# First layer of a four-layer graph network: the attention product and the probability transposes change places in TensorE's order

## The reference

```python
q = split_heads(x @ Wq.T + bq)          # H = 8 heads of 32
k = split_heads(x @ Wk.T + bk)
v = split_heads(x @ Wv.T + bv)
scores = jnp.einsum('bhsd,bhtd->bhst', q, k) * SCALE
scores = jnp.where(mask, scores, jnp.float32(-1000000000.0))   # 6 static masks, 2 of adj
attn = jax.nn.softmax(scores, axis=-1)
out = jnp.einsum('bhst,bhtd->bhsd', attn, v)
out = out.transpose(0, 2, 1, 3).reshape(Bn, S, D)
return out @ Wo.T + bo
```

## Time and profile before

| | us |
|---|---|
| median of 3 runs (lowest, highest) | 2136.47 (2135.16, 2137.15) |
| the profiled execution | 2136.92 |
| its span, first to last instruction | 2135.0 |
| TensorE busy in the span | 2034.9 (95%) |
| VectorE busy | 1514.9 (71%) |
| ScalarE busy | 1001.2 (47%) |
| GpSimd busy | 566.6 (27%) |

### The profile page before, as it was taken

How to read it: one execution, slowest core, us unless ns; L and a number is a source line. 1 busy time by engine, 2 the same in 40 slices (tenths; PEclk the granted TensorE clock), 3 DMA queues, 4 the chain that set the end, 5 groups by cost and what they waited for, 6 DMA issues and landing times. The chain is left out here.

```text
span 2135.0 us, 52810 instructions
## 1 busy us (share of the span) xinstructions
PE 2034.9 (95%) x18428; PEld 1882.9 (88%) x18428; DVE 1514.9 (71%) x3344; ACT 1001.2 (47%) x2057; POOL 566.6 (27%) x624
## 2 busy tenths in 40 slices
PE   7999999899999799999999999999998899999997
PEld 6888888899998699999999999999998778887886
DVE  7899999677777455555555555555554799999997
ACT  6667666455555322232222232233222567666765
POOL 4344444222222011101111111111111444444442
PEclk9999999999999899999999999999999999999999
DMA  3222222432323200011111111001110122112211
GB/s 104 69 75 70 66 75 75 148 90 82 89 77 90 73 16 26 22 30 30 30 30 30 30 30 30 21 24 30 30 30 21 42 61 60 51 55 60 60 45 45
DMA packets 149370, 113.31 MB, mean 53 GB/s; under 512 B 42944, under 2 KB 148800, under 8 KB 149312
## 3 DMA queue, kind: packets, MB, share of 16 engines
q1 hardware_dynamic: 149312, 112.52, 18.2%
HBM read 78.93 MB, written 33.55 MB: 53 GB/s over the span
## 5 line engine op out<-in xcount | busy, mean ns | idle before, releaser
L273 POOL TENSOR_TENSOR ln_rstd<-ln_var_eps,minus_half 128x2 f32<-128x2 f32 x128 | 90.8, 709 | 904.6 <-DVE ln_var_eps L266 904.6
L1693 ACT ACTIVATE l_cat_hi<-banks 128x512 fp32r<-128x512 f32 x128 | 76.5, 597 | 261.6 <-PE banks L1866 261.6
L161 PE MATMUL banks<-ln_hT_hi,square_w_hi 128*128 128x256 f32 x512 | 155.5, 304 | 5.0 <-DVE square_w_lo L638 3.2
L161 PE MATMUL banks<-ln_hT_hi,l_g_w_hi 128*128 128x256 f32 x512 | 148.6, 290 | 4.9 <-POOL l_a_bd L1646 4.9
L290 ACT ACTIVATE ln_h<-ln_x,ln_shift,ln_rstd 128x256 f32<-128x256 f32 x256 | 139.5, 592 | 28.7 <-DVE ln_shift L280 23.7
L163 PE MATMUL banks<-ln_hT_hi,square_w_lo 128*128 128x256 f32 x512 | 146.2, 285 | 0.0
L162 PE MATMUL banks<-ln_hT_lo,square_w_hi 128*128 128x256 f32 x512 | 146.1, 285 | 0.0
L161 PE MATMUL banks<-l_cat_hi,l_aw_hi 128*128 128x256 f32 x512 | 144.2, 282 | 1.4 <-DVE l_cat_lo L1753 1.4
L163 PE MATMUL banks<-l_cat_hi,l_aw_lo 128*128 128x256 f32 x512 | 144.1, 281 | 0.0
L162 PE MATMUL banks<-l_cat_lo,l_aw_hi 128*128 128x256 f32 x512 | 143.8, 281 | 0.0
L163 PE MATMUL banks<-ln_hT_hi,l_g_w_lo 128*128 128x256 f32 x512 | 142.8, 279 | 0.0
(11 more groups left out here) (234 smaller groups left out, 6984.6 us busy)
## 6 DMA issues: line engine op xcount, KB each, us to landing
hidden<-y SPq DMA_DIRECT2D x96, 256.0 KB, 2.2
ln_x<-hidden SPq DMA_DIRECT2D x96, 256.0 KB, 2.8
x_res<-hidden SPq DMA_DIRECT2D x96, 256.0 KB, 2.9
ln_x<-x SPq DMA_DIRECT2D x32, 256.0 KB, 2.8
x_res<-x SPq DMA_DIRECT2D x32, 256.0 KB, 3.0
out<-y SPq DMA_DIRECT2D x32, 256.0 KB, 2.2
l_adj_u<-adj SPq DMA_DIRECT2D x96, 16.0 KB, 2.4
l_stage_attnT<-L_attnT SPq DMA_DIRECT2D x4, 256.0 KB, 3.2
```

Source lines behind the costliest of these rows:

```text
L161: nc.tensor.matmul(out, lhs(lh), rhs(rh), start=start, stop=False, skip_group_check=True)
L273: self.nc.gpsimd.tensor_tensor(self.rstd[:, g.slot], self.var_eps[:, g.slot], self.core.minus_half[:, 0:PAIRS], ALU.pow).then_inc(self.rst ...
L1693: nc.scalar.activation(cat_hi[:, h * KC:(h + 1) * KC], halves(B_HP[h]), ACT.Relu).then_inc(cat_hi_ready.sem, 1)
```

## The change

In the first layer, the attention product of a group leaves the end of its step and moves into the next step, between that step's first and second score tile (`attend`). The layer norm's transposes now come right behind `values`, and the probability transposes behind them, at the end of the step. These go into banks 7 (unused before) and 6 (shared with the attention product, hence the wait for `oT_lo_ready`) in place of 4 and 5; the score tiles wait for `shifted_ready` of the group before in place of `probT_ready`. The lists of the other engines are as they were. In the second layer (not `direct`) the order is the old one.

```diff
--- before.py
+++ after.py
@@ -428,7 +428,7 @@
         B_OT = 6 if direct else 0
         B_Q, B_K, B_V, B_PROJ = 1, 2, 1, 3
         B_S, B_O = 4, 6
-        B_PT = [4, 5] if NT == 2 else [5]
+        B_PT = [7, 6] if direct else [5]
         w_loaded = core.once("setup_loaded_" + tag)
         hi_split = core.once("setup_hi_" + tag)
         lo_split = core.once("setup_lo_" + tag)
@@ -788,19 +788,35 @@
             def step(g):
                 gn = ln.group(g)
                 c2, b1, e = g.back(2), g.back(1), g.back(3)
+                def attend(a):
+                    u = a.slot
+                    after(pe, v_act_ready, a)
+                    after(pe, v_dve_ready, a)
+                    after(pe, probT_ready, a)
+                    for p in range(PAIRS):
+                        for b in range(2):
+                            for j in range(HH):
+                                r0, col = (j % 2) * S, (j // 2) * TOK + (2 * p + b) * S
+                                last = nc.tensor.matmul(
+                                    ps[r0:r0 + S, B_OT, col:col + S], v_bd[:, u, p, b, j].rearrange("q a e -> q (a e)"),
+                                    probT[:, u, p, j, b * S:(b + 1) * S], start=True, stop=True,
+                                    skip_group_check=True)
+                    last.then_inc(oT_in_psum.sem, 1)
+
+                if direct and e.exists(groups) and not c2.exists(groups):
+                    attend(e)
                 if c2.exists(groups):
                     u = c2.slot
                     for t in range(NT):
 
+                        if t == 1 and direct and e.exists(groups):
+                            attend(e)
                         if t == 0:
                             after(pe, mask_ready, c2)
                             after(pe, q_ready, c2)
                             after(pe, k_bd_act_ready, c2)
                             after(pe, k_bd_dve_ready, c2)
-                        if NT == 2:
-                            after(pe, probT_ready, c2.back(1), t + 1)
-                        else:
-                            after(pe, shifted_ready, c2.back(1))
+                        after(pe, shifted_ready, c2.back(1), t + 1)
                         if static_mask is not None:
                             w0 = static_mask.shape[1]
                             for r in halves_of_rows:
@@ -880,42 +896,31 @@
                     project_out()
                 if b1.exists(groups):
                     values()
-                if direct and c2.exists(groups):
-                    for t in range(NT):
-                        transpose_prob(weighted, weighted_ready, t)
                 if gn is not None:
                     if direct:
                         after(pe, ln.hT_lo_ready, gn.back(1))
                     else:
                         after(pe, oT_lo_ready, gn.back(3))
                     ln.transpose(pe, gn, B_HT)
-                if c2.exists(groups):
+                if direct and c2.exists(groups):
+                    after(pe, probT_ready, c2.back(1))
+                    after(pe, oT_lo_ready, e)
+                    for t in range(NT):
+                        transpose_prob(weighted, weighted_ready, t)
+                if not direct and c2.exists(groups):
                     u = c2.slot
                     after(pe, v_act_ready, c2)
                     after(pe, v_dve_ready, c2)
-                    if not direct:
-                        after(pe, probT_ready, c2)
-                        after(pe, o_ready, c2.back(1))
-                        for p in range(PAIRS):
-                            for b in range(2):
-                                for j in range(HH):
-                                    last = nc.tensor.matmul(
-                                        ps[b * S:(b + 1) * S, B_O + p, j * 2 * VW:(j + 1) * 2 * VW],
-                                        probT[:, u, p // TP, (p % TP) * HH + j, b * S:(b + 1) * S],
-                                        v_bd[:, u, p, b, j], start=True, stop=True, skip_group_check=True)
-                        last.then_inc(o_in_psum.sem, 1)
-                    else:
-                        after(pe, oT_lo_ready, c2.back(1))
-                        for p in range(PAIRS):
-                            after(pe, probT_ready, c2, p + 1)
-                            for b in range(2):
-                                for j in range(HH):
-                                    r0, col = (j % 2) * S, (j // 2) * TOK + (2 * p + b) * S
-                                    last = nc.tensor.matmul(
-                                        ps[r0:r0 + S, B_OT, col:col + S], v_bd[:, u, p, b, j].rearrange("q a e -> q (a e)"),
-                                        probT[:, u, p, j, b * S:(b + 1) * S], start=True, stop=True,
-                                        skip_group_check=True)
-                        last.then_inc(oT_in_psum.sem, 1)
+                    after(pe, probT_ready, c2)
+                    after(pe, o_ready, c2.back(1))
+                    for p in range(PAIRS):
+                        for b in range(2):
+                            for j in range(HH):
+                                last = nc.tensor.matmul(
+                                    ps[b * S:(b + 1) * S, B_O + p, j * 2 * VW:(j + 1) * 2 * VW],
+                                    probT[:, u, p // TP, (p % TP) * HH + j, b * S:(b + 1) * S],
+                                    v_bd[:, u, p, b, j], start=True, stop=True, skip_group_check=True)
+                    last.then_inc(o_in_psum.sem, 1)
 
             run_steps(pe, step, groups, 3)
     core.end_layer(used)
```

## The result

| | before | changed |
|---|---|---|
| median, us (lowest, highest; runs) | 2136.36 (2135.16, 2137.15; 4) | 2156.68 (2155.8, 2156.72; 4) |
| profiled execution's span | 2135.0 | 2154.8 |
| a step in the loop, mean of 23 | 11.27 | 11.88 |

The changed kernel is slower, by a ratio of 1.0095 (95% interval 1.0077 to 1.0112), +20.3 us on the medians. The prediction said 2159 us, with a range of 2148 to 2171.

What follows compares the result with a forecast made beforehand. It took VectorE and the ln_x load that its y releases as the bound, 11.27 us a step. Terms 16.2 + 1.8 + 3.6 + 0.5 = 22.1 us on the profiled 2136.92, adjusted to the median, gave 2159, range 2148 to 2171.

Steps and rivals of the forecast that it cites:

- The ring: First layer's loop: from second exponential through ln_h, transposes, probT copies and ln_hT_hi to the next; 11.97 us, +0.70 a step.
- Into the loop: Three steps up to the loop's start: bounded by something else, VectorE waiting for its load; 0 taken, 3 us at most.
- The drain: Last step with a softmax: layer norm's transposes pass in front of both probability tiles, with the work behind exposed; 0.5 us.
- the product behind the first score tile: Attention product one step later on TensorE: ScalarE's l_oT_hi late by under 1 us of 2.92 idle; cost 0.
- TensorE's round: TensorE's own work over a step: it waits about 1 us per step and isn't the bound.
- the waits that went: Score tiles' wait for probT and TensorE's 0.34 us stall for l_weighted bring nothing; VectorE's wait for ln_x goes too.
- TensorE is the bound: Rival: TensorE bounds the first layer's step, so its 0.34 us stall going counts, 10.9 us faster, 2126; 6 in 100.
- The slack takes it: Rival: copies slip only by the transposes' 0.55 us, 0.41 of it into the load wait; 2137 to 2141; 7 in 100.
- The clock falls: Rival: TensorE's pause each step drops its clock until the projections, slowing scores and product; 67 us on top, 2226; 3 in 100.

Runs made afterwards that it cites:

- before_early_load: Kernel before, with SyncE issuing the store of y behind the next step's load of ln_x in the first layer: 2118.97 us, ratio 0.9934.
- the early load: SyncE edit, first layer: store of y issued behind the next step's load of ln_x; on the changed kernel 2153.57 us, ratio to the kernel before 1.0101.
- lnT_first_only: Kernel before with only the layer norm's transposes moved ahead of the probability transposes, attention product left in place: 2153.05 us, ratio 1.0077.
- lnT_last: Changed kernel with the layer norm's transposes back behind the probability transposes, attention product still moved: 2135.27 us, ratio to the kernel before 0.9996.
- hT_hi_first: Changed kernel with ScalarE copying ln_hT_hi ahead of the two probT copies: 2137.98 us, ratio to the kernel before 1.0009.

## Why the prediction was right, step by step

2159 us were predicted and 2156.68 measured, and the mechanism is the one that was named. Three terms outside the loop were wrong and happened to cancel, which is luck.

**The ring** held link by link. From the rows of the changed kernel above, beside what was put down:

| link | predicted | measured |
|---|---|---|
| second exponential to end of `ln_h` | 3.30 | 3.30 |
| to the layer norm's transposes | 0.15 | 0.05 |
| to the first probability tile (taken between 0.49 and 0.60) | 0.55 | 0.49 |
| to probT | 0.69 | 0.68, mean of the loop's two halves (0.64 in the step shown, 0.72 in the next) |
| two copies, to `ln_hT_hi` | 0.97 | 0.97 |
| to `ln_hT_lo` | 0.63 | 0.71 |
| to the statistics | 0.61 | 0.61 |
| to the next second exponential, mean of two | 5.07 | 5.07 (5.20 in the step shown, 4.93 in the next) |
| sum | 11.97 | 11.88, and 11.88 by 23 steps |

The links taken from rows of the loop itself were right to 0.01 us. The hand-overs between engines had been taken from steps outside the loop, where a waiting engine could be seen, and the transposes' 0.55 was chosen between two bounds; these were off by up to 0.1 each, and together they made the step 0.1 too long, 2 us over the loop.

**The sum by stretches**, from the statistics of the earlier trace rows and their counterparts:

| stretch | before | changed | predicted | measured |
|---|---|---|---|---|
| to the third step's statistics | 23.24 | 22.00 | 0 | -1.2 |
| three steps before the loop | 30.36 | 33.77 | +3.6 | +3.4 |
| into the loop, three | 36.62 | 35.26 | 0 | -1.4 |
| in the loop, 23 | 259.11 | 273.24 | +16.2 | +14.1 |
| last two | 21.78 | 23.22 | +1.8 | +1.4 |
| last statistics to the layer's last y | 14.14 | 17.27 | +0.5 | +3.1 |

The sum is 19.4 of the 19.8 us by which the spans differ. Outside the loop three terms missed, by -1.2, -1.4 and +2.6 us. That they cancel is luck; what is left of the miss is the loop's 2.1 us. *Into the loop*: put at 0 because the load was the bound there, which before_early_load confirms (31.9 us with the load out of the way). The changed kernel's steps take about what the ring takes (35.26, against 35.5 worked out), so they got shorter. Why the load was late there in the kernel before is open. *The start*: both kernels do the same work there, but TensorE's products of one kind took 0.41 us each until 18.2 us in the kernel before, and only until 15.5 us in the changed one, then 0.28. 0.41 is what they take in the drain at 1.2 GHz, and 0.28 at 2.4, though the record of the granted clock reads 1.00 in this stretch. It isn't the change's doing: these statistics come at 21.51 to 23.24 us in the ten traces, at 22.00 in the changed kernel and at 23.05 in the same order with the early load. The kernel before and the changed one:

```profile
17.54 0.41 PE L161 MATMUL banks<-ln_hT_hi,l_w_hi 128*128 128x256 f32 x1
```

```profile
16.26 0.28 PE L161 MATMUL banks<-ln_hT_hi,l_w_hi 128*128 128x256 f32 x1
```

*The drain*: mostly the clock, see the rivals; and its 0.5 was laid to the wrong one of the two moves. From the last statistics to `l_oT_hi` it took 9.89 us in the kernel before and 9.88 in lnT_first_only, so the transposes' new order is free there. With the product moved it took 10.30 in lnT_last and 10.36 in the changed kernel with the early load, with the granted clock at 1.00 up to there in all four: the moved product waits for both probT copies, where before it started after the first.

```profile
377.48 0.84 ACT L558 ACTIVATE l_oT_hi<-banks,l_b_col 128x256 fp32r<-128x256 f32 x2 [0.84 <-PE banks L800]
```

(lnT_last, whose last statistics start at 367.18.)

**What was said to cost nothing** cost nothing in the loop: the product behind the first score tile (lnT_last), TensorE's round (a pause of 1.28 us, "about 1 us" predicted), the waits that went. The product's 0.4 to 0.5 us in the drain is the one exception.

**The rivals.** "TensorE is the bound": no; hT_hi_first keeps TensorE's new order and a pause of 0.71 us a step, and is at the time before. "The slack takes it": 0.41 us of it did, and the rest remained. "The clock falls": not in the loop, at a pause of 1.28 us with twelve transposes behind it, in every one of 23 steps. The granted clock from 91 to 364 us is 1.00, and the lengths of the products, which showed the slow start where that record didn't, agree: those of L162 take 0.28 us in all of these steps, none over 0.29.

```profile
91.00:364.00 273.00, 243.52 (x2670) 221.30 (x2668) 232.56 (x553) 176.10 (x391) 108.99 (x138) 1.00 0.24 68
389.00:391.00 2.00, 0.08 (x1) 0.11 (x2) 1.97 (x5) 0.63 (x1) 0.50 (x1) 1.00 0.00 0
391.00:393.00 2.00, 2.00 (x10) 2.00 (x11) 1.93 (x6) 0.63 (x1) 0.00 (x0) 0.52 0.00 0
395.00:397.00 2.00, 2.00 (x10) 1.73 (x9) 0.00 (x0) 0.60 (x1) 1.32 (x2) 0.50 0.39 131
```

(Busy us by engine with counts, then granted clock, DMA share, GB/s.) The Trainium skill, "TensorE: Matmul & The Clock Gate", section "Part 4: PE-mode transpose", says that transposes don't count as TensorE's activity in the way that matmuls do. The loop neither confirms nor refutes that: the clock held, but each step also has its matmuls. The clock did fall in the drain, in the other three rows above: TensorE had next to nothing from 389 to 391 us, and from 391 its granted clock was 0.50, the level of 1.2 GHz, through the last transposes, product and projection. `l_oT_hi` comes 12.43 us after the last statistics there, 2.1 us later than in the changed kernel with the early load (10.36). So of the +3.1 some 0.5 is the moved product and the rest the clock. In lnT_first_only, with the same ring, the clock stays up until 407 us and the same stretch takes 403.01 - 389.52 = 13.49, 3.8 us less than in the changed kernel. It had reached that stretch 2.0 us later, so 1.8 us less are left at the layer's end; against the kernel before on their own chips the two stand at +17.3 and +20.3 us. These medians are of several runs, of which one has a trace, so how much of their 3.0 us is the clock isn't shown.

```profile
389.52 0.74 DVE L255 BATCH_NORM_STATS2 ln_stats<-ln_x 128x6 f32<-128x256 f32 x2
...
403.01 0.69 DVE L708 TENSOR_TENSOR y<-banks,l_x_bo 128x512 f32<-128x512 f32 x1 [1.86 <-issue]
...
396.37 0.63 PE L298 MATMUL banks<-constants_sb,ln_h 128*128 128x128 f32 x4 [1.75 <-ACT ln_h L290]
...
396.83 1.04 PE L858 MATMUL banks<-constants_sb,l_weighted 128*128 128x128 f32 x8
```

The kernel before had a pause of 2.17 us in its last softmax step too and kept its clock there (it fell at 383.6, for its last projection). Whether the changed order makes the fall likelier isn't settled by these runs; in the changed kernel with the early load it fell only between 400 and 401, and the stretch took 15.2.

## What to carry to other kernels

When an instruction is moved ahead in an engine's queue, ask when its input is ready, not how long it takes: four transposes of 0.6 us, put in front of others that were ready, held them for 1.3 us. Then follow who copies what is held back, in order, until it comes back to its start; the sum of the links is the step, and an engine at 95% that waits for others isn't the bound. Give the consumer the order of the producer (`ln_hT_hi` ahead of probT) and the same move costs nothing that can be told from the noise, as long as the step is longer than TensorE's own work and its pause; and a store that waits for a result shouldn't stand in a queue ahead of the next load.

## What the runs showed of the hardware that was not expected

- Four transposes of 128x128 f32 occupy TensorE for 0.49 us until the next may start. A waiting ScalarE starts its copy 0.64 to 0.72 us after the start of the probability transposes, and 0.75 us after that of the layer norm's (165.38 to 166.13). The end of `ln_h` on ScalarE reaches a waiting TensorE in 0.05 us inside the loop (158.80 to 158.85) and in 0.15 us outside it (396.22 to 396.37 in lnT_first_only); this is where the prediction's link was 0.10 too long.
- The clock's fall in the drain costs some 3 us in one kernel and nothing in its neighbour (17.27, 15.21 and 13.49 us for the same work, 0.5 of it the moved product in the first two), which is as much as some edits bring. Terms of a drain should carry it in their range.
